# A transformer layer on one core: the normalised rows turned through device memory and VectorE, one chain for both deviations, and the maxima's rows on ScalarE's queue

## What is computed

```python
q = (route @ wq + bq).reshape(b_, r_, k_, H, D)   # k and v likewise
scores = jnp.einsum('brkhd,brnhd->brknh', q, k) / D ** 0.5
attn = jax.nn.softmax(scores, axis=3)
out = jnp.einsum('brknh,brnhd->brkhd', attn, v).reshape(b_, r_, k_, m_)
out = out @ wo + bo
x = _layernorm(route + out, ln1_g, ln1_b)
ff = jax.nn.relu(x @ w1 + b1) @ w2 + b2
return _layernorm(x + ff, ln2_g, ln2_b)
```

## Time and profile before

| | us |
|---|---|
| median of 3 runs | 4288.4 (4286.61 to 4296.82) |
| the profiled execution | 4295.68 |
| its span | 4293.6 |

### The profile page before, as it was taken

One profiled execution on the slowest core, in us unless ns is written; L12 is line 12 of the kernel. 1 busy time (PEld: TensorE's weight loads), 2 busy tenths in 40 slices (PEclk: granted clock), 3 DMA queues, 4 the chain that ended last, 5 costly groups with the idle time before them and its releaser, 6 DMA issues.

```text
span 4293.6 us, 151787 instructions
## 1 busy us (share of the span) xinstructions
PE 4178.0 (97%) x50954; PEld 3638.6 (85%) x50954; DVE 3694.2 (86%) x9739; ACT 3424.5 (80%) x5889; POOL 3616.9 (84%) x4620
## 2 busy tenths in 40 slices
PE   5999999999999999999999999999999999999998
PEld 4888888888888888888888888888888888888886
DVE  5888888888888888888888888888888888888886
ACT  3888887878888887888888877888887888888886
POOL 4888888888888888888888888888888888888887
PEclk8999999999999999999999999999999999999999
DMA  5555655555656565555555555555565556555562
GB/s 124 145 148 146 154 144 149 146 141 147 153 141 154 145 152 145 145 148 150 148 146 152 147 141 148 144 149 151 144 155 138 149 145 155 146 150 148 146 154 59
DMA packets 1294636, 621.92 MB, mean 145 GB/s; under 512 B 636544, under 2 KB 1293696, under 8 KB 1293824
## 3 DMA queue, kind: packets, MB, share of 16 engines
q1 hardware_dynamic: 1024016, 477.81, 45.7%
q10 hardware_dynamic: 269808, 133.99, 10.7%
HBM read 135.40 MB, written 67.11 MB: 47 GB/s over the span
## 4 chain that ended last, share of the span: by engine, by line
PE 77%; SPq 9%; issue 5%; DMA 3%; DVE 3%; ACT 2%; POOL 2%; ACTq 0%; DVEq 0%; POOLq 0%
PE s_ps L681 10%; PE oT_ps L708 10%; PE bankB L667 10%; PE bankC L646 9%; PE bankC L667 9%; PE sT_ps L695 9%; SPq L246 7%; PE bankB L646 7%; PE bankA L721 5%; PE bankA L771 4%; DMA stack<-parts 3%; PE bankA L646 3%; PE bankB L640 2%; SPq L240 2%; PE oT_ps L764 1%
## 5 line engine op out<-in xcount | busy, mean ns | idle before, releaser
L398 ACT ACTIVATE prob_sb<-sT_ps 128x1024 f32<-128x1024 f32 x1024 | 1044.2, 1020 | 610.9 <-PE sT_ps L695 595.1
L511 DVE TENSOR_REDUCE max_sb<-s_ps 128x8 f32<-128x1024 f32 x1024 | 1213.2, 1185 | 17.0 <-PE s_ps L681 14.6
L271 POOL TENSOR_TENSOR parts<-rest_sb,parts 128x512 bf16<-128x512 f32 x512 | 585.8, 1166 | 223.5 <-ACT parts L372 223.5
L681 PEld LDWEIGHTS s_ps<-stack 96*128 96x128 bf16 x8192 | 463.8, 98 | 307.9 <-issue 243.3
L681 PE MATMUL s_ps<-stack 96*128 96x128 bf16 x8192 | 639.6, 221 | 54.3 <-DMA stack<-parts 25.7
L695 PE MATMUL sT_ps<-stack 99*128 99x128 bf16 x8192 | 629.0, 219 | 1.3 <-ACT prob_sb L398 1.3
L708 PE MATMUL oT_ps<-prob_sb,v_ones 128*32 128x128 f32 x16384 | 553.6, 276 | 3.0 <-ACT prob_sb L398 2.2
L667 PE MATMUL bankB<-w_sb,h_sb 128*128 128x128 f32 x4096 | 525.4, 281 | 7.3 <-ACT h_sb L379 6.6
L708 PEld LDWEIGHTS oT_ps<-prob_sb,v_ones 128*32 128x32 f32 x16384 | 416.3, 109 | 128.2 <-DVE max_parts L609 69.2
L695 PEld LDWEIGHTS sT_ps<-stack 99*128 99x128 bf16 x8192 | 504.3, 98 | 3.0 <-ACT prob_sb L398 1.8
L667 PE MATMUL bankC<-w_sb,h_sb 128*128 128x128 f32 x4096 | 499.2, 275 | 0.0
(11 more groups left out here) (78 smaller groups left out, 8721.1 us busy)
## 6 DMA issues: line engine op xcount, KB each, us to landing
stack<-parts SPq DMA_DIRECT2D x3072, 128.0 KB, 2.6
x_blocks<-in_x SPq DMA_DIRECT2D x1024, 64.0 KB, 2.1
out<-out_sb ACTq DMA_DIRECT2D x256, 256.0 KB, 3.5
x_sb<-in_x ACTq DMA_DIRECT2D x255, 256.0 KB, 3.1
stack<-max_parts SPq DMA_DIRECT2D x768, 8.0 KB, 3.1
w_sb<-in_L_conv_w SPq DMA_DIRECT2D x2, 256.0 KB, 3.0
x_sb<-in_x SPq DMA_DIRECT2D x1, 256.0 KB, 3.1
be_row<-in_L_conv_ln_b SPq DMA_DIRECT2D x2, 64.0 KB, 5.3
```

The lines of the kernel that those rows point to most:

```text
L271: pool.tensor_tensor(parts[:, r % 2, 3 * c + LO], rest_sb[:, c], parts[:, r % 2, 3 * c + MID], ALU.subtract).then_inc(lo_split, 1)
L398: act.activation(prob_sb[:, s % 2], sT_ps[:], ACT.Exp, scale=float(D) ** -0.5).then_inc(exp_done, 1)
L511: dve.reduce_max(max_sb[:, (r - lag) % 2, :, s], s_ps[:].rearrange("p (h k) -> p h k", h=H), AX.X).then_inc(max_done, 1)
L681: ins = pe.matmul(s_ps[:, h * P:(h + 1) * P], stack[0:PROD, (r - lag) % 4, 0, h, tok], stack[0:PROD, (r - lag) % 4, 1, h, tok], start=True ...
```

## The change

- The rows n_sb are no longer transposed on TensorE. SyncE stores them to device memory (`n_mem`), waits for that store, and loads them back in blocks of 32 columns; VectorE's block transpose makes `nT_sb`. ScalarE takes the high part of it, GpSimd (no longer VectorE) the rest. All that follows comes one step later: first hidden chunks at lag 6, the others and the way down at lag 7, output at lag 8.
- One chain of GpSimd operations, on 8 numbers a row, makes the deviations of both norms in a step (the first norm of lag 5, the second of lag 8). ScalarE's four output activations stand together, behind the high part of x; the four of the first norm stand ahead of it.
- The three transfers of the maxima's rows are issued by ScalarE, between its first and second relu at the end of the step, behind a wait for the parts.
- The loop has 120 steps a turn and 12 steps ahead of it (two turns).
- At the start: the memsets of the stack's ones write float32 pairs and one of them is VectorE's; x's first block transpose comes before the weights' split; ScalarE loads wo and bv, and does one exponential first.

The diff, cut to its core (eight leading blanks are cut from each line):

```diff
-UNROLL = 48
-LEAD = 8
+UNROLL = 120
+LEAD = 12
 DMA = 16
...
+        if live(t, r, 5):
+            sp.wait_ge(n_done, upto(t, r, 5, plus=1))
+            sp.dma_start(n_mem[(r - 5) % 2].rearrange("(s k) m -> k s m", s=SEQS), n_sb[:]).then_inc(n_stored, DMA)
         if live(t, r, -1):
             if (v := upto(t, r, 0)) is not None:
                 sp.wait_ge(x_turned, v)
             load_blocks(t + (r + 1), r + 1)
-        if live(t, r, 2):
-            sp.wait_ge(max_parts_made, upto(t, r, 2, plus=1))
-            for part in range(MAXROWS):
-                sp.dma_start(stack[PROD + part:PROD + part + 1, (r - 2) % 4, 0],
-                             max_parts[:, part]).then_inc(max_rows_loaded, DMA)
+        if live(t, r, 5):
+            sp.wait_ge(n_stored, upto(t, r, 5, per=DMA, plus=DMA))
+            for j in range(P // BLK):
+                sp.dma_start(n_blocks[j * BLK:(j + 1) * BLK].rearrange("q (t c) -> q t c", c=BLK),
+                             n_mem[(r - 5) % 2].rearrange("(t q) (j c) -> j q t c", q=BLK, c=BLK)[j]).then_inc(n_blocks_loaded, DMA)
         if live(t, r, 0):
             for c, order in enumerate((Q_PARTS, K_PARTS)):
                 sp.wait_ge(lo_split, upto(t, r, 0, per=2, plus=c + 1))
                     sp.dma_start(stack[j:PROD:len(Q_PARTS), r % 4, c].rearrange("d h x -> d (h x)"),
                                  parts[:, r % 2, 3 * c + part]).then_inc(stack_loaded[r % 2], DMA)
-    iterate(sp, step, 0, LEAD, LAST, 7)
...
+            if live(t, r, 5):
+                pool.wait_ge(mv1_done, upto(t, r, 5, plus=1))
+            if live(t, r, 8):
+                pool.wait_ge(mv2_done, upto(t, r, 8, plus=1))
             if (v := upto(t, r, 5)) is not None:
                 pool.wait_ge(n_done, v)
-            pool.tensor_tensor(minus_m1[:], mv1[:, :, 0], minus_one[:], ALU.mult)
-            pool.tensor_tensor(ve1[:], mv1[:, :, 1], eps_sb[:], ALU.add).then_inc(ve1_done, 1)
-            pool.wait_ge(ve1_done, upto(t, r, 5, plus=1))
-            pool.tensor_tensor(rs1[:], ve1[:], minus_half[:], ALU.pow).then_inc(rs1_done, 1)
-            pool.wait_ge(rs1_done, upto(t, r, 5, plus=1))
-            pool.tensor_tensor(shift1[:], minus_m1[:], rs1[:], ALU.mult).then_inc(shift1_done, 1)
+            if (v := upto(t, r, 9, per=2, plus=2)) is not None:
+                pool.wait_ge(m_done, v)
+            pool.tensor_tensor(minus_m[:], mv[:, :, :, 0], minus_one[:], ALU.mult)
+            pool.tensor_tensor(ve[:], mv[:, :, :, 1], eps_sb[:], ALU.add).then_inc(ve_done, 1)
+            pool.wait_ge(ve_done, upto_chain(t, r))
+            pool.tensor_tensor(rs[:], ve[:], minus_half[:], ALU.pow).then_inc(rs_done, 1)
+            pool.wait_ge(rs_done, upto_chain(t, r))
+            pool.tensor_tensor(shift[:], minus_m[:], rs[:], ALU.mult).then_inc(shift_done, 1)
+        if live(t, r, 6):
+            pool.wait_ge(nT_hi, upto(t, r, 6, plus=1))
+            if (v := upto(t, r, 6, per=FC)) is not None:
+                pool.wait_ge(f1_done, v)
+            pool.tensor_tensor(nT_parts[:, REST], nT_sb[:], nT_parts[:, HI].bitcast(F32), ALU.subtract).then_inc(nT_lo, 1)
         if live(t, r, 4):
...
                 pool.wait_ge(z_done, v)
...
-            pool.wait_ge(m_done, upto(t, r, 7, per=2, plus=2))
-            if (v := upto(t, r, 7)) is not None:
+        if live(t, r, 8):
+            pool.wait_ge(m_done, upto(t, r, 8, per=2, plus=2))
+            if (v := upto(t, r, 8)) is not None:
                 pool.wait_ge(out_ready, v)
             pool.tensor_tensor(mg_sb[:], m_sb[:], each_seq(g2_row), ALU.mult).then_inc(mg_done, 1)
-            pool.wait_ge(mg_done, upto(t, r, 7, plus=1))
-            if (v := upto_dma(t, r, 7, before=1)) is not None:
-                pool.wait_ge(out_stored[(r - 7) % 2], v)
-            pool.tensor_tensor(out_sb[:, (r - 7) % 2], mg_sb[:], each_seq(be2_row), ALU.add).then_inc(out_ready, 1)
-        if live(t, r, 6):
-            pool.wait_ge(mv2_done, upto(t, r, 6, plus=1))
-            if (v := upto(t, r, 6, per=2)) is not None:
-                pool.wait_ge(m_done, v)
-            pool.tensor_tensor(minus_m2[:], mv2[:, :, 0], minus_one[:], ALU.mult)
-            pool.tensor_tensor(ve2[:], mv2[:, :, 1], eps_sb[:], ALU.add).then_inc(ve2_done, 1)
-            pool.wait_ge(ve2_done, upto(t, r, 6, plus=1))
-            pool.tensor_tensor(rs2[:], ve2[:], minus_half[:], ALU.pow).then_inc(rs2_done, 1)
-            pool.wait_ge(rs2_done, upto(t, r, 6, plus=1))
-            pool.tensor_tensor(shift2[:], minus_m2[:], rs2[:], ALU.mult).then_inc(shift2_done, 1)
         if live(t, r, 4):
             normalise(t, r, 1)
+        if live(t, r, 8):
+            pool.wait_ge(mg_done, upto(t, r, 8, plus=1))
+            if (v := upto_dma(t, r, 8, before=1)) is not None:
+                pool.wait_ge(out_stored[(r - 8) % 2], v)
+            pool.tensor_tensor(out_sb[:, (r - 8) % 2], mg_sb[:], each_seq(be2_row), ALU.add).then_inc(out_ready, 1)
         if live(t, r, 0):
             lo_part(t, r, 0)
             lo_part(t, r, 1)
...
+    def apply2(t, r, lag):
+        act.wait_ge(shift_done, upto_chain(t, r))
         if (v := upto(t, r, lag)) is not None:
             act.wait_ge(mg_done, v)
-        for s in (2 * half, 2 * half + 1):
-            ins = act.activation(m_sb[:, s], y_sb[:, s], ACT.Identity, bias=shift2[:, s:s + 1],
-                                 scale=rs2[:, s:s + 1])
-        ins.then_inc(m_done, 1)
...
+            relu(t, r, 7, 2)
+            relu(t, r, 7, 3)
+        exponentials(t, r, 1)
         if live(t, r, 6):
-            relu(t, r, 6, 2)
-            relu(t, r, 6, 3)
-        exponentials(t, r, 1)
-        if live(t, r, 7):
-            apply2(t, r, 7, 1)
+            act.wait_ge(n_turned, upto(t, r, 6, plus=1))
+            if (v := upto(t, r, 6, per=FC)) is not None:
+                act.wait_ge(f1_done, v)
+            if (v := upto(t, r, 6)) is not None:
+                act.wait_ge(nT_lo, v)
+            act.activation(nT_parts[:, HI], nT_sb[:], ACT.Copy).then_inc(nT_hi, 1)
+        if live(t, r, 5):
+            act.wait_ge(shift_done, upto_chain(t, r))
+            if (v := upto(t, r, 5)) is not None:
+                act.wait_ge(x1g_done, v)
+            for s in range(SEQS):
+                ins = act.activation(n_sb[:, s], z_sb[:, s], ACT.Identity, bias=shift[:, 0, s:s + 1],
+                                     scale=rs[:, 0, s:s + 1])
+            ins.then_inc(n_done, 1)
         if live(t, r, 0):
             act.wait_ge(x_turned, upto(t, r, 0, plus=1))
             if (v := upto(t, r, 0)) is not None:
                 act.wait_ge(k_done, v)
             act.activation(xT_parts[:, HI], xT_sb[:], ACT.Copy).then_inc(xT_hi, 1)
-        if live(t, r, 5):
-            act.wait_ge(shift1_done, upto(t, r, 5, plus=1))
-            if (v := upto(t, r, 5)) is not None:
-                act.wait_ge(nT_done, v)
-            if (v := upto(t, r, 5)) is not None:
-                act.wait_ge(x1g_done, v)
-            for s in range(SEQS):
-                ins = act.activation(n_sb[:, s], z_sb[:, s], ACT.Identity, bias=shift1[:, s:s + 1],
-                                     scale=rs1[:, s:s + 1])
-            ins.then_inc(n_done, 1)
+        if live(t, r, 8):
+            apply2(t, r, 8)
...
         exponentials(t, r, 2)
-        if live(t, r, 5):
-            act.wait_ge(nT_done, upto(t, r, 5, plus=1))
-            if (v := upto(t, r, 5, per=FC)) is not None:
-                act.wait_ge(f1_done, v)
-            act.activation(nT_parts[:, HI], B[:], ACT.Copy).then_inc(nT_hi, 1)
...
-        if live(t, r, 5):
-            relu(t, r, 5, 0)
-            relu(t, r, 5, 1)
+        if live(t, r, 6):
+            relu(t, r, 6, 0)
+        if live(t, r, 2):
+            act.wait_ge(max_parts_made, upto(t, r, 2, plus=1))
+            for part in range(MAXROWS):
+                act.dma_start(stack[PROD + part:PROD + part + 1, (r - 2) % 4, 0],
+                              max_parts[:, part]).then_inc(max_rows_loaded, DMA)
+        if live(t, r, 6):
+            relu(t, r, 6, 1)
         if live(t, r, 0):
...
-    act.wait_ge(consts_set, N_SET)
+        if live(t, r, 8):
+            act.wait_ge(out_ready, upto(t, r, 8, plus=1))
+            act.dma_start(out_g[t + (r - 8)], out_sb[:, (r - 8) % 2]).then_inc(out_stored[(r - 8) % 2], DMA)
...
+    dve.memset(stack[PROD:PROD + MAXROWS, 0:2, 1].bitcast(F32), TWO_ONES).then_inc(stack_ones_set, 1)
+    def turn_x(t, r):
+        dve.wait_ge(blocks_loaded[r % 2], upto_dma(t, r, 0, per=P // BLK * DMA))
+        if (v := upto(t, r, 0)) is not None:
+            dve.wait_ge(v_done, v)
+        if (v := upto(t, r, 0)) is not None:
+            dve.wait_ge(xT_lo, v)
+        dve.transpose(xT_sb[:], x_blocks[:, r % 2]).then_inc(x_turned, 1)
+    turn_x(0, 0)
...
+            dve.wait_ge(n_blocks_loaded, upto(t, r, 6, per=P // BLK * DMA, plus=P // BLK * DMA))
+            if (v := upto(t, r, 6)) is not None:
```

(23 more changed lines are left out.)

175 lines of the change are left out of this document (85 added, 90 removed).

## The result

The changed kernel takes 4498.5 us (median of 4 runs, 4491.22 to 4502.73) where the kernel before takes 4288.4: a ratio of 1.0484, 95% interval 1.0465 to 1.0503. It is 4.8% slower. The profiled execution took 4491.22 us, its span is 4489.4, and TensorE's granted clock in it was 0.993 of full speed (0.994 before; both the 2.4 GHz level), so the clock explains nothing. By the profiled executions the spans differ by 196 us, by the medians 210: the profiled run lay 7.3 us over the median before and 7.3 us under it after. The forecast was 4355 and its range ended at 4450: the sign and the place were right, the size was not.

A forecast was written before the change was run, and what follows sets the result against it. TensorE's order of work bounds the kernel. 245 steps x (16.58 - 16.15) = +105, stack waits -20, edges -15, start -12, end +9: +67 us on 4288.4 gives 4355 us; range 4190 to 4450.

The forecast's parts named there:

- Chain one: ScalarE's row issues, second relu and copy of v, then TensorE's projection: ends late, step 16.58 us instead of 15.70.
- Short issues: Rival: ScalarE issues each row in 0.44 us; step 16.08 us, 4233 us in all; chance 0.14.
- the saving is kept: Rival: ScalarE's queue takes the row issues as if free; step 15.70 us, 4140 us in all; chance 0.17.
- The locked generator: Rival: descriptor generation serves one sequencer at a time, lengthening row issues that meet SyncE's; 4801 us; chance 0.03.
- The trip through memory: Rival: the normalised rows' store lands late and TensorE waits; 4355 to 4400 us; chance 0.08.
- Stack waits: TensorE's waits for the stack's transfers, 25.7 us in total, of which 20 us were expected to go.
- edges: Edges between loop turns: one in place of four, each worth 4.95 us, together -15 us.
- start: Before TensorE's first product, a wait of 17.40 us: work cut or moved there was put at -12 us.
- end: Last group pays a store's and a load's landing, issues and the turn in the open: +9 us.
- chain two: GpSimd's shared deviations, ScalarE's normalisations and high part, GpSimd's rest of x, TensorE's products: 0.2 us slack, hidden by chain one.
- power by element: Rival: GpSimd's power on 8 numbers takes 1.84 us, third exponential 0.37 us late; step 16.95, 4446 us; chance 0.12.

The follow-up runs named there:

- fastest variant: Changed kernel with two row issues behind ScalarE's first exponential, the third behind the relus of lag 7, and x turned and split first: 4174.3 us (0.9722).
- dose series: Changed kernel with 0, 1, 2 or 3 row issues left between the relus, the others elsewhere on ScalarE: 4251.7, 4247.7, 4303.7, 4498.5 us.

## Why the prediction came out as it did

Right, with the numbers of the clean step above (times since the projection before it):

- *TensorE bounds the kernel, and a step without the transposes and with nothing late is 0.45 us shorter.* The fastest variant has 0.40 of it, as far as it can be told apart from the rest of its order of work.
- *Chain one, the debt between the relus.* From the first split to the first issue 3.33 us (3.31 forecast), three issues 1.81 (1.82), start of the relu 0.10 (0.11), relu to copy 0.59 (0.57), copy 0.59 (0.60). Each term held within 0.02, and the dose series shows that it is this chain that costs.
- *Short issues* fell with 0.53 + 1.25 us; *the saving is kept* fell with 251 waits.
- *The locked generator* would have made the step 18.4 us; it was 17.16. The Trainium skill, page "Perfetto Trace Analysis", section "DMA Instruction — HWDGE (DVE, Sync)", has a sequencer wait for the other's descriptor generation. With SyncE's transfers held back, the row issues kept median and maximum, so here the wait within their duration is not for SyncE.
- *The trip through memory* decides nothing by landing late: 4.2 us of stack waits, and 11.6 with the stack 2 us later. The trip counts through SyncE's queue instead, full as soon as the rows return to it. The forecast's 14.4 us of issues are 14.6 in the changed kernel's step from 2010.37 on (0.60, 3.10 and 2.00 for the trip and the blocks, 8.92 for the stack).
- *Stack waits* -21.5 us (-20), *edges* -23 us (16 to 30) as a part by itself (-15), *start* -9.7 (-12), *end* +9.9 (+9).

Wrong, and why 4355 became 4498. The forecast amounts to 67 us; the profiles differ by 196. Two terms were too small.

- *The price of the power, and with it what chain one starts from.* On 8 numbers it took 1.65 us. I had the bounds 1.02 and 1.84, and took the middle, 1.43, where "chain one, which still ends later, hides both". It doesn't: chain two feeds chain one. x's rest starts at 8.02, the products at 9.35 (9.05 forecast), and the first split, which the forecast let start at 10.10 as soon as the exponential ends, now waits for the product and starts at 10.36. The dear power reaches the split by a second way too: the third exponential stands behind the four output activations and starts at 9.39, not at 9.18, and without the wait for the product the split would by my estimate have come only 0.05 us earlier (an exponential's start to the next activation is 0.91 to 0.92 us where nothing else holds it). That is +0.26 us into chain one's start, and cutting the power in two gave back 0.29 us a step. With 0.07 us more from the copy's end to TensorE (0.14, not 0.07) and 0.01 of the other terms together the clean step is 16.92 and not 16.58: 0.34 x 255 = 87 us. The rival *power by element* (16.95) had this step nearly right, and I gave it 0.12.
- *The length of three issues is not their usual length.* 1.82 us was one step's row, and the maximum of 1930 ns stood in the same place. Counted over the timeline from 120 to 4080 us, three issues took on average 2.06 us from the first's start to the last's end in the kernel before, on SyncE, where it cost nothing, and 2.04 in the changed one. On a chain that TensorE waits for, the mean counts: the wait for v was 0.83 us on average and 0.57 in the clean step. In that stretch of the changed kernel, the step across the loop's edge and its neighbour left out, 157 steps with issues of the usual length (under 1.86 us, on average 1.82) took 16.97 us and the other 71 (2.54) took 17.67. The length of a step follows that of its three issues with a slope of 0.97 and a correlation of 0.95. Beside fewer stack waits and edges than in the kernel before, the mean step lies 0.24 over the clean one; the forecast's sum, +70 us in the steps, has 16.66, 0.08 over its clean one. The difference, 0.15 x 255, is 39 us.

Together 126 of the missing 129 us; the other 3 are start and end, which were put at -3 and came to 0. The top of the range, 4450, was the price of a dear power with usual issues; it took in a bad case for one term but not for the mean of another.

What made the change slow is then the three issues between the relus (247 us less with all three elsewhere) and, behind them, the dear power ahead of x's rest (-81 us when cut in two; with the rows elsewhere, taking x first gave -77). Both terms are worked out from the traces of the runs named; no run has issues of one length. Not shown by itself is what the trip through memory is worth without the order of work that the fastest variant has. And the mechanism that makes some issues long stays open: it is not SyncE's issues beside them, and it is not ScalarE's queue alone, since SyncE's row issues have it too (to 1.93 us, and 1.94 on ScalarE). The 13 traces do show when it happens. Of the 5373 issues that either queue started 2 us or more after the end of its own last one, not one took over 0.61 us; of the 68672 that started within 0.5 us of it, 11 of 100 took over 0.8 us (all from 120 to 4080 us). So it goes with what the same queue has just issued. In the changed kernel the first row issue has such a pause ahead of it (0.53 to 0.57 us), and the two behind it have not. That is a count over traces; no run was made in which only the spacing changes.

## What to carry to other kernels

A DMA issue on a compute engine's queue is an instruction of that engine: before moving it, find what stands behind it in program order and how long before its need that ends, and split the issues over several places so that each gets no more than its slack. Two chains of which one "hides" the other must be followed to where one feeds the other's start. Where a term lies on the path, take its mean over the whole trace, not the value of one clean step, and compare a clean step with a clean one.

## What the runs showed of the hardware

- GpSimd's power on 128x4 took 1.017 us and on 128x8 1.647 us: 0.157 us per number of a row and 0.39 fixed, worked out from the two.
- An issue of a row of 8 KB took 0.53 us as a rule as the first of a group in the changed kernel and about 0.6 after another; in 27 of 100 steps (SyncE, kernel before) to 31 (ScalarE, with SyncE silent) a group of two or three took over a quarter longer than its shortest.
- In the changed kernel the x load's issue on ScalarE, behind the rows, reached 1.54 us (median 0.43), where it never passed 0.442 us before.
- From the end of ScalarE's copy of v to the start of the waiting TensorE it was 0.144 to 0.146 us in all 251 waits of the changed kernel, twice what the forecast had.
- A DMA issue on ScalarE's or SyncE's queue was long only close behind another one of the same queue: none of 5373 that came 2 us or more behind took over 0.61 us, and 11 of 100 of those within 0.5 us took over 0.8 us (up to 3.4; all 13 traces, 120 to 4080 us).
